# Layer 1 of a four-layer network: more query and key products ahead of the threshold search, and routing masks laid out by expert with a partition's rows adjacent

## The reference, cut to what matters

```python
cap = int(CAP_FACTOR * T / E)                      # 1.25 * 4096 / 32 = 160
probs = jax.nn.softmax(h @ r2_w.T, -1)
topp, topi = jax.lax.top_k(probs, TOPK)            # TOPK = 2
hit = topi[..., None] == eids
routed = hit.any(1)
score = jnp.where(routed, probs, -jnp.inf)
idx = jnp.argsort(-score, axis=0)[:cap].T
xe = xf[idx]
```

```python
q = (x @ Wq.T + bq).reshape(b, l, H, HD).transpose(0, 2, 1, 3)
k = (x @ Wk.T + bk).reshape(b, l, H, HD).transpose(0, 2, 1, 3)
v = (x @ Wv.T + bv).reshape(b, l, H, HD).transpose(0, 2, 1, 3)
q = _apply_rope(q, cos, sin)
k = _apply_rope(k, cos, sin)
```

## Time and profile before

| | us |
|---|---|
| median of three runs | 2280.9 |
| the profiled execution, its own time | 2283.21 |
| its span in the trace | 2281.3 |
| busy in the span: PE / VectorE / ScalarE / GpSimd | 1918.8 / 1669.8 / 1221.0 / 517.9 |
| mean granted clock of TensorE | 0.91 |

### The profile page before, as it was taken

The page is one execution under the profiler, slowest core; times in us unless marked ns, Lnnn a source line. Parts: engine busy times, 40 slices in busy tenths (PEclk is TensorE's granted clock), DMA queues, the critical chain, the costliest instruction groups (busy, mean ns, idle before and its releaser), DMA issues. The chain is left out here.

```text
span 2281.3 us, 45278 instructions
## 1 busy us (share of the span) xinstructions
PE 1918.8 (84%) x17589; PEld 991.8 (43%) x17589; DVE 1669.8 (73%) x2861; ACT 1221.0 (54%) x2473; POOL 517.9 (23%) x602
## 2 busy tenths in 40 slices
PE   2888877866647999999978899999897988697899
PEld 1222221443211337943342377766443455565554
DVE  5999999685779996579854755537675887685665
ACT  3999999332324884368854255555342031184433
POOL 1112110012674551134425533320100000001100
PEclk7898999987776999999988899999998999987999
DMA  8423420100642524624211122220124242000000
GB/s 276 84 56 84 84 56 1 74 18 6 152 165 39 126 44 120 189 56 78 31 22 56 58 66 65 63 97 1 62 91 128 82 118 73 8 1 27 1 19 19
DMA packets 150333, 159.39 MB, mean 70 GB/s; under 512 B 53580, under 2 KB 123030, under 8 KB 150114
## 3 DMA queue, kind: packets, MB, share of 16 engines
q1 hardware_dynamic: 139880, 140.43, 22.7%
q0 software_dynamic: 10240, 16.06, 3.2%
HBM read 87.53 MB, written 72.82 MB: 70 GB/s over the span
## 5 line engine op out<-in xcount | busy, mean ns | idle before, releaser
L435 ACT ACTIVATE a_E<-a_scores,a_nmax 128x512 f32<-128x512 f32 x512 | 343.2, 814 | 14.6 <-DVE a_nmax L368 13.7
L1014 ACT ACTIVATE a_E<-a_scores 128x512 f32<-128x512 f32 x512 | 273.5, 601 | 96.4 <-PE a_scores L1049 91.3
L368 DVE TENSOR_REDUCE a_nmax<-a_scores 128x2 f32<-128x1024 f32 x256 | 302.6, 1217 | 21.8 <-PE a_scores L450 18.1
L918 DVE TENSOR_REDUCE a_nmax<-a_first 128x2 f32<-128x1024 f32 x256 | 295.5, 1217 | 15.2 <-PE a_first L1039 14.1
L450 PE MATMUL a_scores<-a_Vh,a_Kh 48*128 48x512 bf16 x512 | 108.2, 421 | 96.5 <-ACT a_E L435 71.9
L1039 PE MATMUL a_first<-a_Kh,a_Qh 48*128 48x512 bf16 x512 | 148.1, 416 | 36.9 <-PEq L51 20.1
L463 PE MATMUL a_turn<-a_E,a_QS 128*32 128x256 f32 x2048 | 174.1, 416 | 2.3 <-DVE a_QS L378 1.8
L435 ACT ACTIVATION_READ_ACCUMULATOR a_E<-a_scores,a_nmax 128x1 f32 x512 | 167.1, 335 | 0.0
L1049 PE MATMUL a_scores<-a_Qh,a_Kh 51*128 51x512 bf16 x512 | 160.7, 394 | 5.1 <-PEq L51 1.9
L1071 PE MATMUL a_out<-a_E,a_V 128*32 128x256 f32 x2048 | 161.7, 396 | 0.0
L450 PEld LDWEIGHTS a_scores<-a_Vh,a_Kh 48*128 48x128 bf16 x512 | 24.9, 94 | 216.5 <-ACT a_E L435 179.1
(11 more groups left out here) (546 smaller groups left out, 4409.4 us busy)
## 6 DMA issues: line engine op xcount, KB each, us to landing
f_up<-in_L_up SPq DMA_DIRECT2D x32, 256.0 KB, 3.3
a_Kh<-a_rows_k SPq DMA_DIRECT2D x16, 384.0 KB, 6.3
a_Vh<-a_rows_v SPq DMA_DIRECT2D x16, 384.0 KB, 9.8
a_Qh<-a_rows_q SPq DMA_DIRECT2D x32, 192.0 KB, 5.1
a_Kh<-a_rows_k SPq DMA_DIRECT2D x32, 192.0 KB, 6.1
slots<-empty SPq DMA_DIRECT2D x8, 645.0 KB, 6.4
f_xe<-slots SPq DMA_DIRECT2D x40, 129.0 KB, 2.0
outs<-zeros SPq DMA_DIRECT2D x8, 512.0 KB, 5.8
```

The lines of the kernel that those rows point to most:

```text
L368: v.tensor_reduce(nmax[:, rd % 2, r1, :, q], bank(b, u)[:], AX.X, ALU.max, negate=True).then_inc(S["max_ready"], 1)
L435: m = a.activation(E[:, u % NE, x], bank(b, u)[:, x], ACT.Exp, bias=nmax[:, rd % 2, r1, x, q:q + 1], accum_out=Z[:, rd % 2, r1, x, q:q + 1])
L918: v.tensor_reduce(out, slot_bank(n)[:], AX.X, ALU.max, negate=True).then_inc(S["slot_read"], 1)
L1014: a.activation(E[:, u % NE, x], ps_s[n % 3][:], ACT.Exp, scale=SCALE).then_inc(S["exp_ready"], 1)
```

## The change

It sets EARLY to 14. PE then runs products 0 to 13 in the softmax block, step i of the search has product 14 + i up to i = 25, and neither the last four steps nor the place after them has one. VectorE's, ScalarE's and GpSimd's lists for the projection stay as they are.

The masks, the counts in PSUM, `kept` and the positions are laid out as (b e r): for each batch and expert the partition's four rows are adjacent. The probabilities and the hit masks stay as (b r e). So the masks are written with a hop of four elements, summed over adjacent elements, and read by PE with the hop; the count products write PSUM with a hop of four f32; the products with the hit masks read the positions with it. The sums are written as bf16 by the reduction itself, and the two copies to bf16 are gone.

```diff
-        EARLY = 9
+        EARLY = 14
...
-            posn = room[:, 0:2].rearrange("p b t -> p (b t)").rearrange("p (t e) -> p t e", e=NE)
-            above, equal = (eqm[:].bitcast(BF16)[:, n * LQ:(n + 1) * LQ].rearrange("p (b r e) -> p b r e", b=NB, r=R)
+            posn = room[:, 0:2].rearrange("p b t -> p (b t)")
+            posn_rows = posn.rearrange("p (b e r) -> p b r e", b=NB, r=R)
+            above_flat, equal_flat = (eqm[:].bitcast(BF16)[:, n * LQ:(n + 1) * LQ] for n in range(2))
+            above, equal = (eqm[:].bitcast(BF16)[:, n * LQ:(n + 1) * LQ].rearrange("p (b e r) -> p b r e", b=NB, r=R)
                             for n in range(2))
...
-            kept = k3.sb("f1_kept", [128, NB, R, NE], BF16)
-            sums = k3.sb("f1_sums", [128, NB, NE])
+            kept = k3.sb("f1_kept", [128, NB, NE, R], BF16)
+            P4 = P[:].rearrange("p (b r) e -> p b r e", r=R)
...
-            above_ps = [ps_d[:, c].rearrange("p r x -> p (r x)").rearrange("p (b r e) -> p b r e", b=CH, r=R) for c in range(2)]
-            equal_ps = [J["banks"][c][:].rearrange("p (b r e) -> p b r e", b=CH, r=R) for c in range(2)]
+            above_ps = [ps_d[:, c].rearrange("p r x -> p (r x)").rearrange("p (b e r) -> p b r e", b=CH, r=R) for c in range(2)]
+            equal_ps = [J["banks"][c][:].rearrange("p (b e r) -> p b r e", b=CH, r=R) for c in range(2)]
...
-                    v.tensor_tensor(above_rows, P[:], ps_c[:, 1, 0:NE].unsqueeze(1).broadcast_to(SH), ALU.is_gt)
-                    v.drain()
-                    v.tensor_reduce(sums[:], above.rearrange("p b r e -> p b e r"), AX.X, ALU.add)
-                    v.drain()
-                    v.tensor_copy(sum_above[:], sums[:]).then_inc(S["above_ready"], 1)
+                    v.tensor_tensor(above, P4, ps_c[:, 1, 0:NE].unsqueeze(1).unsqueeze(1).broadcast_to([128, NB, R, NE]), ALU.is_gt)
+                    v.drain()
+                    with nc.allow_low_precision(reason="whole numbers up to four are exact in 16 bits"):
+                        v.tensor_reduce(sum_above[:], above.rearrange("p b r e -> p b e r"), AX.X, ALU.add
+                                        ).then_inc(S["above_ready"], 1)
...
-                    v.tensor_tensor(kept_rows, kept_rows, above_rows, ALU.add)
-                    v.drain()
-                    v.tensor_tensor(posn, posn, kept_rows, ALU.mult)
-                    v.drain()
                     for n in range(2):
-                        v.tensor_tensor(hits[n][:], hits[n][:], posn, ALU.mult)
+                        rows = hits[n][:].rearrange("p (b r) e -> p b r e", r=R)
+                        v.tensor_tensor(rows, rows, posn_rows, ALU.mult)
                         v.drain()
                         v.tensor_reduce(slot[:, n], hits[n][:], AX.X, ALU.add)
...
                     for i in range(30):
                         pe.wait_ge(S["count_ready"], i + 1)
                         pe.matmul(ps_c[:, 0, 0:1], fold_half[:], cnt_half[:], start=True, stop=True).then_inc(S["folded"], 1)
-                        product(pe, EARLY + i)
-                    product(pe, 5 * NB - 1)
+                        if EARLY + i < 5 * NB:
+                            product(pe, EARLY + i)
```

More of the change, by code:

```diff
@@ L1467, in route1 @@
             SQ, eqm = (k3.sb(f"f1_{n}", [128, LQ]) for n in ("SQ", "eqm"))
-            posn = room[:, 0:2].rearrange("p b t -> p (b t)").rearrange("p (t e) -> p t e", e=NE)
-            above, equal = (eqm[:].bitcast(BF16)[:, n * LQ:(n + 1) * LQ].rearrange("p (b r e) -> p b r e", b=NB, r=R)
+            posn = room[:, 0:2].rearrange("p b t -> p (b t)")
+            posn_rows = posn.rearrange("p (b e r) -> p b r e", b=NB, r=R)
+            above_flat, equal_flat = (eqm[:].bitcast(BF16)[:, n * LQ:(n + 1) * LQ] for n in range(2))
+            above, equal = (eqm[:].bitcast(BF16)[:, n * LQ:(n + 1) * LQ].rearrange("p (b e r) -> p b r e", b=NB, r=R)
                             for n in range(2))
-            above_rows, equal_rows = (t.rearrange("p b r e -> p (b r) e") for t in (above, equal))
-            kept = k3.sb("f1_kept", [128, NB, R, NE], BF16)
-            kept_rows = kept[:].rearrange("p b r e -> p (b r) e")
-            sums = k3.sb("f1_sums", [128, NB, NE])
+            kept = k3.sb("f1_kept", [128, NB, NE, R], BF16)
+            P4 = P[:].rearrange("p (b r) e -> p b r e", r=R)
             sum_above, sum_equal = (k3.sb(f"f1_sum_{n}", [128, NB, NE], BF16) for n in ("above", "equal"))
@@ L1567, in _ @@
                     v.wait_ge(S["cand_turned"], 1)
-                    v.tensor_tensor(above_rows, P[:], ps_c[:, 1, 0:NE].unsqueeze(1).broadcast_to(SH), ALU.is_gt)
+                    v.tensor_tensor(above, P4, ps_c[:, 1, 0:NE].unsqueeze(1).unsqueeze(1).broadcast_to([128, NB, R, NE]), ALU.is_gt)
                     v.drain()
-                    v.tensor_reduce(sums[:], above.rearrange("p b r e -> p b e r"), AX.X, ALU.add)
-                    v.drain()
-                    v.tensor_copy(sum_above[:], sums[:]).then_inc(S["above_ready"], 1)
-                    v.tensor_tensor(equal_rows, P[:], ps_c[:, 1, 0:NE].unsqueeze(1).broadcast_to(SH), ALU.is_equal)
+                    with nc.allow_low_precision(reason="whole numbers up to four are exact in 16 bits"):
+                        v.tensor_reduce(sum_above[:], above.rearrange("p b r e -> p b e r"), AX.X, ALU.add
+                                        ).then_inc(S["above_ready"], 1)
+                    v.tensor_tensor(equal, P4, ps_c[:, 1, 0:NE].unsqueeze(1).unsqueeze(1).broadcast_to([128, NB, R, NE]), ALU.is_equal)
                     v.wait_ge(S["totalled"], 1)
@@ L1577, in _ @@
                     v.drain()
-                    v.tensor_reduce(sums[:], equal.rearrange("p b r e -> p b e r"), AX.X, ALU.add)
-                    v.drain()
-                    v.tensor_copy(sum_equal[:], sums[:]).then_inc(S["equal_ready"], 1)
+                    with nc.allow_low_precision(reason="whole numbers up to four are exact in 16 bits"):
+                        v.tensor_reduce(sum_equal[:], equal.rearrange("p b r e -> p b e r"), AX.X, ALU.add
+                                        ).then_inc(S["equal_ready"], 1)
@@ L1581, in _ @@
                     v.wait_ge(S["above_counted"], 1)
                     for c in range(2):
-                        v.tensor_copy(posn[:, c * CH * R:(c + 1) * CH * R].rearrange("p t e -> p (t e)"),
-                                      above_ps[c].rearrange("p b r e -> p (b r e)"))
+                        v.tensor_copy(posn[:, c * T:(c + 1) * T], ps_d[:, c].rearrange("p r x -> p (r x)"))
                     v.wait_ge(S["counted"], 1)
                     v.drain()
+                    kept_flat = kept[:].rearrange("p b e r -> p (b e r)")
@@ L1587, in _ @@
                     for c in range(2):
[L1588 to L1592, removed]
@@ L1593, in _ @@
-                        v.scalar_tensor_tensor(own, equal_ps[c].rearrange("p b r e -> p (b r e)"), 0.0, own, ALU.min, ALU.add)
+                        v.scalar_tensor_tensor(kept_flat[:, c * T:(c + 1) * T], J["banks"][c][:], 0.5,
+                                               equal_flat[:, c * T:(c + 1) * T], ALU.is_lt, ALU.mult)
+                        own = posn[:, c * T:(c + 1) * T]
+                        v.scalar_tensor_tensor(own, J["banks"][c][:], 0.0, own, ALU.min, ALU.add)
                     v.drain()
-                    v.tensor_tensor(kept_rows, kept_rows, above_rows, ALU.add)
+                    v.tensor_tensor(kept_flat, kept_flat, above_flat, ALU.add)
@@ L1596, in _ @@
                     v.drain()
-                    v.tensor_tensor(posn, posn, kept_rows, ALU.mult)
+                    v.tensor_tensor(posn, posn, kept_flat, ALU.mult)
                     v.drain()
                     for n in range(2):
-                        v.tensor_tensor(hits[n][:], hits[n][:], posn, ALU.mult)
+                        rows = hits[n][:].rearrange("p (b r) e -> p b r e", r=R)
+                        v.tensor_tensor(rows, rows, posn_rows, ALU.mult)
                         v.drain()
```

## The result

The changed kernel takes 2304.43 us (median of six runs, 2303.56 to 2306.25), the kernel before 2284.0 in the same comparison: the ratio is 1.009, with a 95% interval of 1.0075 to 1.0105. That is 20.4 us slower, where 5 was forecast; it lies above the range.

What follows compares the result with a forecast made beforehand. Projection spills set the stage's end, with 3.0 us of VectorE slack. VectorE's end: +10.8 - 1.2 - 2.5 + 3.0 - 2.1 = +8.0; less the slack, 5.0 us later: 2286 us, range 2278 to 2299.

Steps and rivals of the forecast that it cites:

- VectorE could end 3 us later: End of the search stage: the projection's last spill sets the end, leaving VectorE 3.0 us of slack.
- The six stalls: Search: PE stands in six value products until the next step's add, VectorE waits; +10.8 us, bounds 9.0 to 14.4.
- The reduction at 1.22 and the cast gone: Mask sums of above: contiguous reduction and no cast, together -2.5 us, bounds -1.8 and -2.5.
- The tail at -2.1: After the count: waits for GpSimd go, positions are read with a hop; -2.1 us, bounds -3.7 and -2.1.
- The projection's chain off the end: Projection: GpSimd ends at 661.5, last landing near 669.5, so it no longer sets the stage's end.
- so GpSimd starts some 14 us earlier: Head of the search block: products 10 and 11 already exist, so GpSimd's wait shortens by some 14 us.
- the start of the search as 0: VectorE's first search step: no shift entered in the sum, 0 us.
- the 1.2 us of the last value product: Just after the search: VectorE no longer waits for the last value product, -1.2 us.
- rival (c): Search: the clock stays low and all six stalls take 2.4 us; +3.6, so 2289.5 us; chance 0.14.
- The hop of the count: Count blocks: PE's strided PSUM writes slow only where the clock was full; +3 us, bounds 0 and +6.7.
- Rival (a): Count blocks: strided PSUM write costs four times per column, +18.8 instead of +3; 2302 us; chance 0.18.
- Writing the masks: VectorE's mask writes with the hop: kept at 1.2 us each, no added cost.

Runs made afterwards that it cites:

- e2_layout: Kernel before with only the by-expert layout and 16-bit sums, nine early products kept: 2287.3 us, ratio 1.0018.
- e3_add_same_step: Changed kernel with each add_v moved one step earlier, into the step whose value product waits for it: 2289.5 us, ratio 1.0019 to the kernel before.
- e7_sums16: Kernel before with both masks' sums written in 16 bits by the reduction and the two copies gone: 2285.2 us, ratio 1.0005.
- e4_conversions: e3_add_same_step with the six small fills moved, three ahead of VectorE's wait for the tables, three to ScalarE: 2286.4 us, ratio 1.001 to the kernel before.
- e5_counts_adjacent: Changed kernel with counts in PSUM, kept and positions by row again, masks still by expert: 2296.3 us, ratio 1.0051 to the kernel before.
- e6_early_sums16: Kernel before with fourteen early products, 16-bit sums in the old layout, same-step adds and fills moved off GpSimd's way: 2276.9 us, ratio 0.9963.

## Why the prediction was wrong, step by step

**Right.** VectorE could end 3 us later before without moving the stage (e2_layout). The six stalls and their cause: e3_add_same_step removes them by moving the add. The reduction at 1.22 and the cast gone. The tail at -2.1, with the products of the hits at 1.97. The projection's chain off the end, though GpSimd ended at 667.85 and not near 661.5.

**The step that failed first: "so GpSimd starts some 14 us earlier" was entered as a gain alone, and the start of the search as 0.** The products themselves did cost nothing in the softmax block: the search block began at 570.26, before at 570.52. But I followed the earlier start of GpSimd along its own chain and never asked which VectorE operations would now lie beside it. The six fills ahead of the search, short and without a neighbour before, met it, although my own figures had GpSimd at work from 573 and the first step at 577: the search started 5.05 us late. The copy L1565 took 2.08 us instead of 0.23 and gave back the 1.2 us of the last value product and more. For it the early products are not the only cause; before, it slipped into a gap of 0.16 us between two GpSimd operations:

```profile
640.91 0.23 DVE L1565 COPY f_cand_rows<-f_cand 128x128 f32<-128x128 f32 x1
...
640.96 2.16 POOL L672 TENSOR_TENSOR a_rest<-a_QK,a_parts 128x1024 f32<-128x1024 f32 x1 [0.16 <-issue]
```

In e7_sums16, with nine early products, it missed that gap and took 1.57 us. That it was cheap before was luck, and a small shift ended it. I had read this wait in the tail (the cast and L1600) and used it there only as a gain. Together 5.05 + 1.85 = 6.9 us of the 14.2 that the sum lacked; e4_conversions shows it for the start, for L1565 the rows alone do. Neither had a term in the sum or in the range; the stalls and the count stayed within their bounds, the count at the very edge.

**The stalls were mis-sized: 10.8 forecast, 13.15 measured.** I took the clock of the value products from the kernel before, two of six at 2.06. After, five take 2.07 or 2.08 us and the sixth 1.83, and each has 2.5 us of PE idleness just before it. In five of the six the granted clock had been 1.00 shortly before and was 0.50 to 0.57 in the value product; the first was at 0.50 all along. I read this as the stall's own doing, but it isn't shown: in e3_add_same_step, with 0.4 to 0.5 us of idleness in their place, three of the six still ran at half clock. In place of 2 x 2.4 + 4 x 1.5 the runs show about 2.2 each. That was my rival (c), priced at +3.6; it came true in part, +2.35.

**The hop of the count was mis-sized: +3 forecast, +6.7 measured,** at the upper bound of the range that I had worked out. The argument that a column at half clock leaves twice as much time is wrong for the write, whose price is in PE's own cycles: 1.64 ns a column against 0.83 at half clock. It holds for the read of the masks, 0.89 against 0.84, which I had not priced. That 6.7 met my bound is luck. Reckoned at the full clock, the two blocks grew from 6.5 x 0.59 + 3.5 = 7.3 us to 9.9 x 0.80 + 7.1 = 15.0, so to twice; the first block was granted 0.80 instead of 0.59 and so hid a part. Rival (a) had the place right and the size wrong, four times instead of twice.

That is where the rule of the Trainium skill, page Advanced Engine Details and Errata (PSUM Cachelines), stood: any non-contiguous pattern slows matmuls significantly. The trace agrees, by a factor of 2.0. PE's read of the masks with a hop of 8 bytes had no term in my sum at all; e5_counts_adjacent shows that it costs a factor of two too, but at the full clock only, and next to nothing where the write is dear already.

**Writing the masks: 0 forecast, +1.2 measured** (2.44 against 1.21). L1231, f32 on 32 partitions, was the wrong row for a 16-bit write on 128. The page Vector Engine (DVE) Microarchitecture Reference of the Trainium skill (Measured stream behaviour on trn2) has up to 2.5 ns a column for a destination that steps each element; its row is for 32-bit words with a step of 24. 2.44 us over 1024 is 2.4, close to it, and my estimate from the page's lower figure, for hops of 4 KiB, was too small.

The 14.2 us between 8.0 and 22.2 are so accounted for by the table's rows: 5.05 for the start, 2.35 for the stalls, 1.85 for L1565, 1.26 for the masks, 3.7 for the count. No rival came true alone. (a) and (c) were right in kind, but each was priced with everything else as forecast, and the neighbours of GpSimd stood in none.

## What to carry to other kernels

When work is moved earlier on one engine, list what each neighbour runs in the newly shared time: an engine that becomes busy sooner can cost its neighbour more than it gains, above all in short operations that stood alone. When a producer is moved ahead by n steps, move what frees its buffer by as much; here one add, one step late, cost 13 us in a queue that runs in order. A layout should be judged on every operand that touches it, reads and writes on each engine: here it made a reduction 0.66 us cheaper, and two engines then wrote at twice the price. Whether a hop hurts can also hang on the clock, so its price should be read at both levels.

## What the runs showed of the hardware that I had not expected

- TensorE pays a factor of two for a hop of four elements between neighbours in the f32 write to PSUM, at full clock (0.83 against 0.43 ns a column) and at half (1.64 against 0.83).
- For the same hop in its bf16 moving operand, the one that streams through, it pays a floor of about 0.88 ns a column: twice the price at full clock (0.42), nearly nothing at half (0.89 against 0.84). With both hops the dearer counts: 0.89 and 1.68.
- VectorE's write of bf16 with that hop costs 2.44 us for 1024 elements instead of 1.21, while a read of f32 with it costs 1.97 instead of 1.23.
- Small operations of 128x128 on VectorE took up to 2.14 and 2.38 us beside a running GpSimd, and 0.22 without it, about as long as a whole GpSimd instruction (2.12 to 2.34). The search's L1555, over 1024 elements, took 1.28 us beside GpSimd and without it. The Trainium skill's GPSIMD Engine Reference (Specifications) names contention with VectorE instructions in a two-port mode or with two SBUF inputs. The trace agrees for two SBUF inputs: the product of the hits took 2.98 us beside GpSimd and 1.23 without (e6_early_sums16). The small casts have one input, and no view here names an operation's mode; e4_conversions gives their price.
